# Perceiver block on one core: expert tiles of two experts' slots of one batch, the first batch's begun while the second is routed

## The reference

```python
cap = int(LOAD * K * max(1, T / E))          # T=512, E=16, K=2: 64 slots per expert and batch
gate_probs = softmax(x @ w_router)
top_k_probs, positions, indices, expert_inputs = vmap(_dispatch)(x, gate_probs)   # per batch
expert_inputs = swapaxes(expert_inputs, 0, 1).reshape(E, B * cap, C)
h = silu(expert_inputs @ w_gate) * (expert_inputs @ w_fc)    # C=512 -> H=256
o = h @ w_proj                                               # H=256 -> C=512
y = vmap(_collect)(o, indices, positions, top_k_probs)       # sum of the two, by their shares
```

## Time and profile before

| | us |
|---|---|
| median of 3 runs | 1996.65 (1996.18 to 1997.01) |
| span of the profiled execution | 1995.1 |
| TensorE busy in it | 1890.6 |
| VectorE, ScalarE, GpSimd busy | 1707.1, 1467.7, 46.2 |
| last tile's counts on TensorE end | 1851.9 |
| first expert's rows are turned from | 1864.14 |
| last expert's copy to `oe` ends | 1963.26 |
| last gather is issued | 1986.21 |

### The profile page before, as it was taken

One profiled execution on the slowest core, in us unless ns is written; L12 is line 12 of the kernel. 1 busy time (PEld: TensorE's weight loads), 2 busy tenths in 40 slices (PEclk: granted clock), 3 DMA queues, 4 the chain that ended last, 5 costly groups with the idle time before them and its releaser, 6 DMA issues.

```text
span 1995.1 us, 31226 instructions
## 1 busy us (share of the span) xinstructions
PE 1890.6 (95%) x11844; PEld 782.4 (39%) x11844; DVE 1707.1 (86%) x1511; ACT 1467.7 (74%) x1671; POOL 46.2 (2%) x57
## 2 busy tenths in 40 slices
PE   7999999999999999999999999999999989998693
PEld 3333333333333333333333333333332446556582
DVE  5799999999999999889999999999996587887354
ACT  2588888888888888778888888888886456553120
POOL 2000000000000000000000000000000000002003
PEclk9999999999999999999999999999999989999797
DMA  7333333333333323322233333333241000008574
GB/s 250 105 95 93 109 90 96 98 103 101 95 91 96 91 80 96 106 80 80 80 85 87 91 86 92 91 89 97 64 120 50 23 1 1 2 1 281 200 259 148
DMA packets 113354, 194.58 MB, mean 98 GB/s; under 512 B 10288, under 2 KB 64560, under 8 KB 113200
## 3 DMA queue, kind: packets, MB, share of 16 engines
q1 hardware_dynamic: 110640, 184.12, 31.5%
q0 software_dynamic: 2560, 8.39, 1.3%
HBM read 109.63 MB, written 50.33 MB: 80 GB/s over the span
## 4 chain that ended last, share of the span: by engine, by line
PE 87%; DVE 6%; issue 2%; ACT 2%; DMA 1%; POOL 1%; POOLq 0%; SPq 0%; DVEq 0%; ACTq 0%
PE ps L1136 23%; PE ps L1330 23%; PE ps L1044 12%; PE ps L1047 12%; PE ps L1389 3%; PE ps L1174 2%; PE ps L1169 2%; PE ps L1070 1%; PE ps L1120 1%; PE ps L1213 1%; PE ps L1399 1%; PE ps L1183 1%; POOL og L1016 1%; DVE dacc L1761 1%; PE ps L1243 1%
## 5 line engine op out<-in xcount | busy, mean ns | idle before, releaser
L1593 ACT ACTIVATE pt<-ps,bias 128x1024 f32<-128x1024 f32 x1024 | 1108.6, 1114 | 212.3 <-PE ps L1330 211.3
L1761 DVE TENSOR_TENSOR dacc<-dacc,pt 128x2048 f32<-128x2048 f32 x496 | 1134.5, 2287 | 60.1 <-ACT pt L1593 36.1
L1330 PE MATMUL ps<-qst,kst 128*128 128x512 f16 x2048 | 611.4, 381 | 7.9 <-ACT pt L1593 7.8
L1136 PE MATMUL ps<-pt,vt 128*32 128x512 f32 x4096 | 493.5, 598 | 0.0
L1330 PEld LDWEIGHTS ps<-qst,kst 128*128 128x128 f16 x2048 | 178.2, 98 | 413.7 <-ACT pt L1593 123.3
L1044 PE MATMUL ps<-wsm 128*128 128x512 f16 x1152 | 312.0, 381 | 10.6 <-DVE wsm L1719 10.6
L1047 PE MATMUL ps<-wsm 128*128 128x512 f16 x1152 | 311.0, 380 | 2.4 <-ACT vt L1444 2.4
L1136 PEld LDWEIGHTS ps<-pt,vt 128*32 128x32 f32 x4096 | 106.9, 109 | 262.6 <-issue 241.1
L1044 PEld LDWEIGHTS ps<-wsm 128*128 128x128 f16 x1152 | 112.9, 98 | 150.0 <-DVE wsm L1719 10.6
L1047 PEld LDWEIGHTS ps<-wsm 128*128 128x128 f16 x1152 | 112.6, 98 | 140.7 <-issue 3.2
L1704 DVE SCALAR_TENSOR_TENSOR wsm<-ps,wsm 128x512 f16<-128x512 f32 x128 | 87.6, 685 | 27.3 <-ACT wsm L1440 27.2
(11 more groups left out here) (215 smaller groups left out, 1205.6 us busy)
## 6 DMA issues: line engine op xcount, KB each, us to landing
kst<-kscr SPq DMA_DIRECT2D x132, 256.0 KB, 3.5
kscr<-wsm SPq DMA_DIRECT2D x128, 256.0 KB, 3.5
kst<-kst SPq DMA_DIRECT2D x124, 256.0 KB, 3.4
wsm<-in_ctx SPq DMA_DIRECT2D x32, 768.0 KB, 5.0
qst<-qscr SPq DMA_DIRECT2D x32, 128.0 KB, 3.0
xbuf<-xn SPq DMA_DIRECT2D x16, 256.0 KB, 3.9
wsm<-in_gate SPq DMA_DIRECT2D x8, 512.0 KB, 4.9
wsm<-in_fc SPq DMA_DIRECT2D x8, 512.0 KB, 5.9
```

The lines of the kernel that those rows point to most:

```text
L1136: p = e.matmul(ps[32 * h:32 * h + 32, 4 + n % 2, :], vt[:, kb % 2, ch, c:c + 32], pt[:, (2 * i + h // 2) % 6, h % 2, :], start=ch == 0, st ...
L1330: p = e.matmul(ps[:, 2 * half + h2, :], kst[:, kb % 2, h, ch * 128:ch * 128 + 128], qst[:, h, :], start=True, stop=True)
L1593: e.activation(pt[:, (2 * i + half) % 6], ps[:, 2 * half:2 * half + 2, :], ACT.Exp, bias=bias[:, 4 * kb + ch:4 * kb + ch + 1], scale=SCORE ...
L1761: e.tensor_tensor(own_heads, own_heads, probs, ALU.add).then_inc(S["add"], 1)
```

## The change

A tile now holds the 64 slots of expert 2p and the 64 of expert 2p+1 of one batch; `TILES` names the sixteen (batch, pair) in their order: three pairs of batch 0, three of batch 1, then mixed. `xbuf` and `obuf` are one per batch, with row numbers of 64 per expert. The first four pairs of batch 0 are read back into `xn3`, behind the first eight scatters. Turning tiles 0 and 1 and `up` of tile 0 stand inside the last tile's routing. Gathers of batch 0 wait for tile 12, those of batch 1 for all.

`e_up` has the slots in the array (64 columns for each of the two experts) and streams gate and fc together, 512 columns; each expert's weights meet only their own 64 slots. The hidden values so come out with slots in the partitions (`hN`) and are turned back by two transposes (`e_back`) and a copy on VectorE (`turned_hidden`). Eight experts' weights have room; pairs of experts follow behind tiles 3, 4, 5 and 7.

```diff
+NW = 8
+TILES = ((0, 0), (0, 1), (0, 2), (1, 0), (1, 1), (1, 2), (0, 3), (1, 3), (0, 4), (1, 4), (0, 5), (0, 6), (0, 7), (1, 5),
+         (1, 6), (1, 7))
+LAST_OF_FIRST = TILES.index((0, 7))
+FOLLOWS = {TILES.index((1, p)): p + 4 for p in range(4)}
...
-    for step in ("x3", "rT", "stat", "rC", "lroot", "lnr", "router", "logit"):
+    out.append(("eturn", 0))
+    for step in ("x3", "rT", "stat", "rC", "lroot", "lnr"):
         follow(7, step)
+    out.append(("eturn", 1))
+    follow(7, "router")
+    out.append(("eup", 0))
+    follow(7, "logit")
...
-            e.wait_ge(S["sct0"], 256)
...
+            e.wait_ge(S["sctA"], 128)
+            rows_load(xn3[:, 0:4, :], 0, 0, 4)
+            e.wait_ge(S["x3"], 8)
+            expert_load(7)
+            rows_load(xe[:, 0:4, :], 0, 4, 8)
+            e.wait_ge(S["sctB"], 128)
+            rows_load(xe[:, 4:7, :], 1, 0, 3)
+            rows_load(xe[:, 7:12, :], 1, 3, 8)
...
+            for t in range(8):
+                if t % 4 == 0:
+                    stored = LAST_OF_FIRST + 1 if t == 0 else 16
+                    e.wait_ge(S["os0"], 16 * ((stored + 1) // 2))
+                    e.wait_ge(S["os1"], 16 * (stored // 2))
+                for k in range(2):
+                    gather(k, t)
...
+            def e_up(x):
...
+                for k in range(4):
+                    for c in range(2):
+                        p = e.matmul(ps[64 * c:64 * c + 64, 6 + s, :].rearrange("p (w n) -> p w n", w=2),
+                                     xeT[:, s, k * 128 + 64 * c:k * 128 + 64 * c + 64], weights(two + c)[0][:, :, k, :],
+                                     start=k == 0, stop=k == 3)
+                p.then_inc(S["up"], 1)
+
+            def e_back(x):
...
+                e.wait_ge(S["hN"], x + 1)
...
+            def e_down(x):
...
+                e.wait_ge(S["hT"], x + 1)
...
-            e_turn(0)
-            for x in range(16):
+            e_up(1)
+            for x in range(1, 16):
                 if x > 1:
+                    e_up(x)
+                e_back(x - 1)
                 if x < 15:
                     e_turn(x + 1)
+                e_down(x - 1)
+            e_back(15)
             e_down(15)
...
+            def turned_hidden(x):
+                s = x % 2
+                e.wait_ge(S["hP"], x + 1)
+                if x > 1:
                     e.wait_ge(S["dn"], x - 1)
+                e.tensor_copy(hT[:, s, :], ps[:, 2, s * 256:s * 256 + 256]).then_inc(S["hT"], 1)
+
+            hidden(0)
+            hidden(1)
+            for x in range(1, 16):
+                turned_hidden(x - 1)
+                if x < 15:
+                    hidden(x + 1)
+            turned_hidden(15)
```

More of the change, by code:

```diff
@@ L687, in build @@
         qscr = nc.dram_tensor("qscr", [8, 128, 2, 512], F16).ap()
-        xbuf = nc.dram_tensor("xbuf", [4096, 512], F32).ap()
-        obuf = nc.dram_tensor("obuf", [2048, 512], F32).ap()
+        xbuf = [nc.dram_tensor(f"xbuf{b}", [3072, 512], F32).ap() for b in range(2)]
+        obuf = [nc.dram_tensor(f"obuf{b}", [1024, 512], F32).ap() for b in range(2)]
         fx = {"q": nc.dram_tensor("fq", [2, 512, 512], F32).ap(),
@@ L935, in expert_load, with rows_load @@
             def expert_load(x):
-                for w, n in zip(weights(x), ("gate", "fc", "proj")):
-                    e.dma_start(w, A[n][x].rearrange("(k p) n -> p k n", p=128)).then_inc(S[f"e{x % NW}"], 16)
+                gate_fc, proj = weights(x)
+                for w, n in ((gate_fc[:, 0], "gate"), (gate_fc[:, 1], "fc"), (proj, "proj")):
+                    e.dma_start(w, A[n][x].rearrange("(k p) n -> p k n", p=128)).then_inc(S[LOADED[x % NW]], 16)
+            def rows_load(to, b, lo, hi):
+                e.dma_start(to, xbuf[b][128 * lo:128 * hi, :].rearrange("(x p) c -> p x c", p=128)
+                            ).then_inc(S[f"qx{part(b, lo)}"], 16)
             e.wait_ge(S["p4"], 8)
@@ new lines, in e_back @@
+            def e_back(x):
+                s = x % 2
+                e.wait_ge(S["hN"], x + 1)
+                if x > 1:
+                    e.wait_ge(S["hT"], x - 1)
+                for i in range(2):
+                    p = e.transpose(ps[:, 2, s * 256 + i * 128:s * 256 + i * 128 + 128],
+                                    hN[:, s, i * 128:i * 128 + 128], ident[:])
+                p.then_inc(S["hP"], 1)
+            def e_down(x):
+                s, two = x % 2, 2 * TILES[x][1]
+                e.wait_ge(S["hT"], x + 1)
+                if x > 1:
+                    e.wait_ge(S["oe"], x - 1)
+                for i in range(2):
+                    for c in range(2):
+                        p = e.matmul(ps[64 * c:64 * c + 64, 3 + s, :], hT[:, s, i * 128 + 64 * c:i * 128 + 64 * c + 64],
+                                     weights(two + c)[1][:, i, :], start=i == 0, stop=i == 1)
+                p.then_inc(S["dn"], 1)
@@ L1468, in act, with e_turn, e_up, e_down @@
             absolute = 0
+            def e_turn(x):
+                s = x % 2
+                e.wait_ge(S["eT"], x + 1)
+                if x > 1:
+                    e.wait_ge(S["up"], x - 1)
+                e.activation(xeT[:, s, :], ps[:, s, :], ACT.Copy).then_inc(S["xeT"], 1)
+            def e_up(x):
+                s = x % 2
+                e.wait_ge(S["up"], x + 1)
+                if x > 1:
+                    e.wait_ge(S["hN"], x - 1)
+                e.activation(sg[:, s, :], ps[:, 6 + s, 0:256], ACT.Exp, scale=-1.0).then_inc(S["sgx"], 1)
+            def e_down(x):
+                s = x % 2
+                e.wait_ge(S["dn"], x + 1)
+                if x > 1:
+                    e.wait_ge(S[f"os{s}"], 16 * (x // 2))
+                e.activation(oe[:, s, :], ps[:, 3 + s, :], ACT.Copy).then_inc(S["oe"], 1)
             def self_piece(ev):
@@ L1473, in self_piece @@
                 i = t % 2
+                if what == "eturn":
+                    e_turn(t)
                 if what == "copy":
@@ L1620, in act @@
             assert ends[0] == ends[1]
-            def e_turn(x):
-                s = x % 2
-                e.wait_ge(S["eT"], x + 1)
+            e_up(0)
+            e_up(1)
+            for x in range(1, 16):
                 if x > 1:
[L1626 to L1639, removed]
-                    e.wait_ge(S[f"os{s}"], 16 * (x // 2))
-                e.activation(oe[:, s, :], ps[:, 6 + s, :], ACT.Copy).then_inc(S["oe"], 1)
-            e_turn(0)
-            for x in range(16):
+                    e_up(x)
                 if x < 15:
                     e_turn(x + 1)
-                e_up(x)
-                if x:
-                    e_down(x - 1)
+                e_down(x - 1)
             e_down(15)
@@ L2106, in dve, with hidden @@
             assert ends[0] == ends[1]
-            for x in range(16):
+            def hidden(x):
                 s = x % 2
```

113 lines of the change are left out of this document (55 added, 58 removed).

## The result

The changed kernel takes 2048.18 us in the median (2045.54 to 2048.89, four runs) against 1996.41 for the kernel before beside it (1995.78 to 1997.01, four runs): a ratio of 1.026, 95% interval 1.0247 to 1.0273. It is 2.6% slower; 2042 was forecast. The profiled execution spans 2046.6 us against 1995.1.

The account below looks back on a forecast made before the run. The prediction took VectorE's chain, laid bare in every tile, to bound the kernel: span 1995.1 + 19.8 for the new order + 25.5 for clock falls = 2040.4 us, plus 1.55 to the median: 2042 us, range 2014 to 2064.

Parts of the forecast that it names:

- What bounds the middle: Sixteen expert tiles: TensorE waits for VectorE's chain in every tile, period 9.13 us against 5.73, TensorE idle 3.3 us in each.
- C(x-1): VectorE's new copy of the turned hidden values of tile x-1 from PSUM, taken as 0.42 us.
- H(x): VectorE's four steps for tile x behind ScalarE's Exp, taken as 2.99 us.
- D(x-1): TensorE's proj of tile x-1, taken as 1.72 us, starting 3.97 us behind the end of U(x).
- U(x): TensorE's gate and fc of tile x, taken as 3.44 us.
- The fifth rival: Tile loop: VectorE's order doesn't hold TensorE, period 5.9 us, no clock falls, 1974 us; chance 0.06.
- Clock: TensorE in the tile loop: half clock behind each of fifteen gaps, 1.7 us each, 25.5 us; bounds 0 and 51.
- The second rival: TensorE's clock holds in the tile loop: 2016.4 us, from 2014 to 2030 with a few falls; chance 0.12.
- the third rival: Gate/fc and proj: the array's halves don't run beside each other, 77 us more, 2119 us; chance 0.08.
- Head: From routing to the first proj: gate and fc of tile 0 delay the counts about 0.2 us; first proj starts at 1860.8.
- Tail: From the last copy to the end: only the second batch's eight gathers left, 21.1 us against 31.8, a gain of 10.7.
- The fourth rival: TensorE's clock, once down, stays down for most of the tile loop: 2067 us and above; chance 0.06.

Follow-up runs that it names:

- the first experiment: The changed kernel with VectorE's copy of hT for tile x-1 put ahead of the four steps of tile x: 1985.04 us, ratio 0.9926 to the kernel before.
- The third: The changed kernel without VectorE's reciprocal, so its output is not the block's: ratio 0.9989 to the kernel before.
- The second experiment: The changed kernel with three unused 512-column f32 matmuls in each tile's TensorE gap: ratio 1.0129 to the kernel before; with one matmul, 1.019.
- the experiment on the head: The kernel with VectorE's copy first, with gate and fc of tile 0 moved behind the second batch's counts: ratio 0.9922 to the kernel before.
- the fourth experiment: The kernel with VectorE's copy first, with the loops of gate/fc and proj turned round, one expert's products before the other's: ratio 1.0039 to the kernel before.

## Why the prediction was right, and by how much it was off

**What bounds the middle: right.** The step that decided was that C(x-1) is queued behind H(x), so that D(x-1) starts only a whole chain behind U(x). The wait is there in every tile with VectorE's write of hT as its releaser, and the first experiment removes it by the order alone. The third, which shortens the chain, shortens the period with it. The fifth rival, that the order doesn't hold TensorE, is refuted for the changed kernel, and its price (1974 us) was about that of the first experiment (1985), with the period 6.26 for 5.9 and the head's wait for rows.

**Period at full clock: 9.22 for 9.13.** The chain from U's end to D's start was put at 3.97 and took 3.82; D and U took 5.40 for 5.16. The two errors have opposite signs, and it is luck that they leave only 0.09 a tile, 1.3 us.

**Clock: the term that was mis-sized.** Fifteen falls at 1.7 us each made 25.5. The second experiment shows the period without falls, so that the falls cost 11.22 - 9.22 = 2.00 us a period, 28.1 in fourteen. From the last but one D to the last it is 4.31 us against 2.82 there, 1.5 more. That makes 29.6, so 4.1 more than forecast. The number of falls was right, and the size of the common one too: ten of the fourteen distances lie between 10.55 and 11.24. The other four are 12.14, 12.09, 12.23 and 12.10 long, one in every three or four: there D takes 3.68 us and U still 4.6 to 4.7 (against 1.94 and 3.46), so that such a fall costs 2.9. The fall from which the 1.7 came was one of 3.4 us. The ratios bear out the greater part of the term: 1.026 against 1.0129 is 26 us, and the kernel with three matmuls has 1.5 us of delay of its own in its last tile. D and U of a short fall (from 1985.2 on), then D and U of a long one (from 1962.0 on), as stretches: length, busy us of TensorE, granted clock, DMA:

```profile
1985.20:1988.60 3.40, 3.40 (x10) 0.51 0.00 0
1988.80:1992.10 3.30, 3.30 (x17) 1.00 0.20 79
```

```profile
1962.00:1965.50 3.50, 3.50 (x10) 0.50 0.00 0
1965.70:1970.20 4.50, 4.50 (x16) 0.74 0.17 62
```

D runs at 0.50, behind the gap; behind this short fall U is at 1.00, behind the long one at 0.74. (Where a short fall begins only within D, its end reaches into U, which then takes 3.9 to 4.1; the cost is the same.) The clock of the gaps themselves, which the profile gives too, shows what is different about the long ones. The first stretch lies ahead of the D at 1961.92, the second ahead of that at 1985.07:

```profile
1961.20:1961.90 0.70, 0.00 (x0) 0.50 0.00 0
1984.30:1984.90 0.60, 0.00 (x0) 1.00 0.00 0
```

Read in steps of 0.1 us, the clock is at half for 6.9 us (from 1961.2 to 1968.1) in a long fall and for 3.5 in a short one. There are five long ones, ahead of D(0) and in the four slow distances, and ten short ones. A fall costs half of what lies over work. In the four slow distances the first 0.7 to 1.1 us of a long one lie in the gap, so that it comes to (6.9 - 1.0) / 2 = 2.95 or so; measured, 12.09 to 12.23 less 9.22, that is 2.87 to 3.01. Ahead of D(0) 2.7 us lay in the gap, which makes 2.1, measured 2.02. A short one comes to 3.5 / 2 = 1.75 at most, measured 1.33 to 1.70. So the term was sized from a short fall, and a third of the falls lasted twice as long.

The second rival (clock holds, 2016) fails as predicted. By the rule of thumb of the Trainium skill, TensorE: Matmul & The Clock Gate, section HAM oscillation, such a gap would be harmless. The trace does not agree, and the measurement decides: here the clock fell behind the gap of about 3.05 us in every tile, and with one added matmul behind nine of fourteen gaps of 2.18 to 2.62. In the tiles with 1.25 and 0.46 it did not.

The length of the gap alone does not decide, though, and what the forecast rested on, that every gap longer than 1.79 us brings a fall, is not borne out: five of those fourteen gaps brought none. That it came out right with fifteen falls for fifteen gaps is in part luck. In the other direction, the clock fell behind gaps of 0.88, 0.97 and 0.96 us one after the other at the end of the experiment on the head (the last D takes 3.43 us), where the first experiment has 0.96, 0.97 and 1.01 and it held (1.94).

**Halves: right for this code,** refuting the third rival (2119), but the fourth experiment shows that it could have been lost by the order of two loops.

**Head: 0.7 late.** D(0) came at 1861.52 for 1860.8, of which 0.5 stands already at the last projection of attention, where this execution was later than that of before (1843.60 against 1843.13). U(0) delayed the counts to 1851.52, as forecast (some 0.2 us against a start of 1850.79 that was itself later here). The second batch's rows were covered, as forecast.

**Tail: 21.05 for 21.1.** Here too two errors cancel, which is luck: 3.2 us to the first gather for 2.82, and 8.5 from the last gather's issue to the end for 8.9.

Sum of the differences: head 0.7, period 1.3, clock 4.1, and 0.1 net for the last tiles' handovers and the tail make 6.2: 2040.4 + 6.2 = 2046.6, the span. The fourth rival (the clock stays down) fails too: between the falls the clock came back to 1.00 every time, and the mean of the stretches of 20 us from 1860 to 1980 lies between 0.74 and 0.84.

## What to carry over

When two tiles are in flight, look at the order on every queue of the loop, not on the busiest engine alone: a short copy for the older tile that stands behind the long chain of the newer one makes the loop serial, and costs the chain in every tile; its place in the program is free. A wait on TensorE has a second price when the clock falls behind it; measure the two apart with matmuls put into the gap. Before covering a step, work out how much of it is not already covered: in the first experiment the copy ended last in the chain of waits, but another piece ran beside it, and only 0.09 us could be gained.

## What was not expected of the hardware

- Work that nobody needs made a kernel faster: three 512-column f32 matmuls in each gap brought 26 us, one brought 14 (ratios 1.0129 and 1.019 against 1.026).
- Of fourteen gaps of 2.18 to 2.62 us the clock fell behind nine and held behind five, equal ones among both. In the changed kernel a third of the falls lasted 6.9 us instead of 3.5 and began while TensorE still idled; the four behind the loop's gaps cost 2.9 us instead of 1.7. What decides between them is open.
- On the array's two column halves products with 64 columns run at the same time even when they don't alternate: with four recorded matmuls in a row on each half there is no loss (1.76 us), with eight 1.77 us are lost. There the second half's first matmul starts together with the fifth of the first half. Other lengths of a row were not run.
- The store of one tile to `obuf` took 2.03 us where no gather was being issued and 4.26 us beside gathers; in both the first store of `out` began under it.
